# Rounding a gate input with a second activation, keeping gates as tanh, and a new order of all operations in a kernel of four blocks

## The reference

```python
# 1 state-space block (mamba), inner width 256, 16 states; it has its own layernorm and residual
h = layernorm(x, gamma, beta); xi, z = split(h @ W_in, 2)
u = silu(causal_conv4(xi) + b_conv)
dt_r, B, C = split(u @ W_x);  dt = softplus(dt_r @ W_dt + b_dt)
s[t] = exp(dt * A) * s[t-1] + dt * u * B[t]        # per channel, for each of 16 states
y = sum_over_states(s * C) + u * Dskip
block = x + (y * silu(z)) @ W_out
# 2 and 4: ffn with ternary weights, inner width 512
block = rmsnorm(gelu(rmsnorm(x) @ w_up_t)) @ w_down_t
# 3 minGRU, inner width 512, between the two ffns
x_in = silu(x @ W1 + b1); x_skip = silu(x @ W2 + b2)
z = sigmoid(x_in @ Wz + bz); ht = x_in @ Wh + bh
h[t] = (1 - z[t]) * h[t-1] + z[t] * ht[t]
block = (x_skip + h) @ Wo + bo
```

## Time and profile before

| | |
|---|---|
| median of 3 runs | 886.41 us (883.97 to 886.82) |
| profiled execution, its own time | 885.23 us |
| its span on the core | 883.4 us |
| PE, busy share of the span | 81% (719.2 us) |
| DVE | 80% (708.4 us) |
| ACT | 71% (629.6 us) |
| POOL | 67% (593.3 us) |
| mean granted TensorE clock | 0.895 |

### The profile page before, as it was taken

The page is one execution under the profiler, slowest core; times in us unless marked ns, Lnnn a source line. Parts: engine busy times, 40 slices in busy tenths (PEclk is TensorE's granted clock), DMA queues, the critical chain, the costliest instruction groups (busy, mean ns, idle before and its releaser), DMA issues. The chain is left out here.

```text
span 883.4 us, 12572 instructions
## 1 busy us (share of the span) xinstructions
PE 719.2 (81%) x4116; PEld 602.6 (68%) x4116; DVE 708.4 (80%) x1092; ACT 629.6 (71%) x942; POOL 593.3 (67%) x374
## 2 busy tenths in 40 slices
PE   5464675679979996999789987999699968997976
PEld 5343463568857785778777876788577857786765
DVE  3579887899979999799989997999799997844231
ACT  4654756678788968897798779887888477526322
POOL 3378847876787869776978787877868567515412
PEclk9755856889979999899989998999899988999995
DMA  2441221111211111121111111121112111000000
GB/s 46 123 168 45 65 60 48 56 42 50 60 47 39 60 45 52 40 71 48 49 50 56 52 55 41 50 61 48 45 42 60 49 36 36 13 1 1 12 1 13
DMA packets 35186, 42.80 MB, mean 48 GB/s; under 512 B 7457, under 2 KB 17074, under 8 KB 35122
## 3 DMA queue, kind: packets, MB, share of 16 engines
q1 hardware_dynamic: 35122, 42.00, 15.9%
HBM read 39.63 MB, written 2.36 MB: 48 GB/s over the span
## 5 line engine op out<-in xcount | busy, mean ns | idle before, releaser
L382 POOL TENSOR_TENSOR inflow<-dtu,b_all 128x1024 f32<-128x1024 f32 x127 | 311.8, 2457 | 121.7 <-DVE state L926 96.2
L1219 PE MATMUL y_ps<-ident,state 128*128 128x128 f32 x1024 | 154.4, 301 | 30.1 <-DVE state L934 30.1
L934 DVE TENSOR_TENSOR state<-state,c_ps 128x1024 f32<-128x1024 f32 x128 | 155.6, 1216 | 25.4 <-PE c_ps L1210 22.2
L1219 PEld LDWEIGHTS y_ps<-ident,state 128*128 128x128 f32 x1024 | 136.1, 157 | 47.4 <-DVE state L934 36.3
L923 DVE TENSOR_TENSOR_SCAN state<-dA,inflow 128x512 f32<-128x512 f32 x128 | 155.7, 1216 | 9.6 <-ACT dA L701 7.9
L926 DVE TENSOR_TENSOR_SCAN state<-dA,inflow 128x512 f32<-128x512 f32 x128 | 153.2, 1197 | 0.0
L701 ACT ACTIVATE dA<-dt,decay_c 128x512 f32<-128x512 f32 x128 | 88.0, 687 | 58.5 <-DVE state L923 50.9
L1114 PE MATMUL work<-in_hi,wzh_hi 128*128 128x512 f32 x256 | 105.9, 414 | 5.6 <-POOL in_lo L537 5.4
L1116 PE MATMUL work<-in_lo,wzh_hi 128*128 128x512 f32 x256 | 101.1, 395 | 0.0
L1115 PE MATMUL work<-in_hi,wzh_lo 128*128 128x512 f32 x256 | 100.8, 394 | 0.0
L703 ACT ACTIVATE dA<-dt,decay_c 128x512 f32<-128x512 f32 x128 | 87.3, 682 | 17.0 <-DVE state L926 16.6
(11 more groups left out here) (163 smaller groups left out, 1582.7 us busy)
## 6 DMA issues: line engine op xcount, KB each, us to landing
b_all<-b_scratch SPq DMA_DIRECT2D x128, 256.0 KB, 3.1
x_tok<-in_x SPq DMA_DIRECT2D x8, 256.0 KB, 3.8
out_x<-x_tok SPq DMA_DIRECT2D x8, 256.0 KB, 3.7
wide<-in_Wz SPq DMA_DIRECT2D x1, 1024.0 KB, 8.0
wide<-in_Wh SPq DMA_DIRECT2D x1, 1024.0 KB, 10.2
skip_f<-in_W SPq DMA_DIRECT2D x2, 256.0 KB, 5.1
dtu<-in_W_in SPq DMA_DIRECT2D x1, 256.0 KB
b_scratch<-gated SPq DMA_DIRECT2D x8, 32.0 KB, 1.6
```

The costliest lines, as they stand in the source:

```text
L382: eng.tensor_tensor(inflow[:, n % 2, :, :], dtu[:, :, :], b_all[:, n % RING, :].unsqueeze(1).broadcast_to([P, HALVES, SEQ]), ALU.mult).the ...
L934: dve.tensor_tensor(state[:, g % 3, :, :], state[:, g % 3, :, :], c_ps[:, :].unsqueeze(1).broadcast_to([P, HALVES, SEQ]), ALU.mult).then_i ...
L1219: last = pe.matmul(y_region(j, h), state[:, g % 3, h, cols(j)], ident[:, :], is_transpose=True, start=False, stop=(n == STATE - 1), skip_g ...
```

## The change

1. **Gate input.** The DVE copy into `in_hi` (32 of them) is gone. ACT runs the silu of `in0` to `in3` a second time, from the same PSUM bank, with the rounded tile as output. The bank is given free after the second. The semaphore `s_inhi` is gone: POOL's `in_lo` waits for the bank's release.
2. **Gates.** The second pass over the gate (32 on ACT) is gone; `gate` holds tanh t. Wh is halved once at the start (4 more ACT passes of 128x512), so that (t+1)*bank is z*(x_in@Wh). `keep` is -0.5t+0.5. The bias bh is taken out of the gated term: the scan starts at -bh instead of 0, and bh@Wo is added once to `bo_tok` (4 small matmuls and one DVE add at the start).
3. **Skip term.** The diagonal matrix (2 DVE instructions) is gone. ACT scales u by Dskip in place (`mix_ud`, 2 passes of 128x512 per unit, after `dtu` and x_dbl have read u), and PE adds it by eight transposes instead of eight matmuls.
4. **Order.** Every table of slots, the table of banks and `MOVED` are new. Unit 1 has exceptions of its own too. The load of x for unit b+2 stands 4 loads of B earlier in SP's queue.
5. Units are now described by (row, from, to, start) so that a unit could be part of a row. All eight are whole rows, so that the slices and the carry that go with it change nothing and no carry is issued.

The core of the diff:

```diff
+UNITS = (
+    (0, 0, 512, 0), (1, 0, 512, 16), (2, 0, 512, 32), (3, 0, 512, 48), (4, 0, 512, 64), (5, 0, 512, 80), (6, 0, 512, 96), (7, 0, 512, 112),
+)
...
             def round_wzh(k):
+                act.activation(wzh_f[:, k, FF:2 * FF], wzh_f[:, k, FF:2 * FF], ACT.Copy, scale=0.5).then_inc(s_halved, 1)
+                act.wait_ge(s_halved, k + 1)
                 act.activation(wzh_hi[:, k, :], wzh_f[:, k, :], ACT.Copy).then_inc(s_hizh, 1)
...
+            def mix_ud(b):
+
+                act.wait_ge(s_dtu, b + 1)
+                full(act, b, "xdbl")
+                for h in range(HALVES):
+                    last = act.activation(u[:, h, tok(b)], u[:, h, tok(b)], ACT.Identity, scale=skip_c[:, h:h + 1])
+                last.then_inc(s_ud, 1)
...
             def gru_in(t, j, r, s):
...
-                    act.activation(in_f[:, j, :], bank(p)[:, :], ACT.Silu, bias=b1_c[:, j:j + 1]
+                    read_by(act, r, s, "h3")
+                    act.activation(in_f[:, j, tok(t)], bank(p)[:, tok(t)], ACT.Silu, bias=b1_c[:, j:j + 1])
+                    act.activation(in_hi[:, j, tok(t)], bank(p)[:, tok(t)], ACT.Silu, bias=b1_c[:, j:j + 1]
                                    ).then_inc(*emptied(p))
...
-                evacuated(act, t, p)
-                act.activation(gate[:, j % 2, :], gate[:, j % 2, :], ACT.Copy, scale=0.5, bias=0.5).then_inc(s_gate1, 1)
...
-            def gru_in_hi(t, j, r, s):
-                evacuated(dve, t, "in%d" % j)
-                read_by(dve, r, s, "h3")
-                dve.tensor_copy(in_hi[:, j, :], in_f[:, j, :]).then_inc(s_inhi, 1)
...
-                dve.scalar_tensor_tensor(mixed[:, j, :], bank(p)[:, :], bh_c[:, j:j + 1], gate[:, j % 2, :],
+                dve.scalar_tensor_tensor(mixed[:, j, tok(t)], gate[:, j % 2, tok(t)], 1.0, bank(p)[:, tok(t)],
                                          ALU.add, ALU.mult).then_inc(*emptied(p))
...
+                first = nbh_c[:, j:j + 1] if FROM[t] == 0 else mixed[:, j, FROM[t] - 1:FROM[t]]
+                dve.tensor_tensor_scan(mixed[:, j, tok(t)], keep[:, j % 2, tok(t)], mixed[:, j, tok(t)], first,
                                        ALU.mult, ALU.add).then_inc(s_hid, 1)
...
-                        last = pe.matmul(y_region(j, h), u[:, h, cols(j)], diag[:, h, :],
+                        last = pe.matmul(y_region(j, h), u[:, h, cols(j)], ident[:, :], is_transpose=True,
                                          start=(j % 2 == 0 and h == 0), stop=False, skip_group_check=True)
```

428 lines of the change are left out of this document (239 added, 189 removed), and 120 rows, old and new, of tables (ACT_AT, BANK, DVE_AT, MOVED).

## The result

The changed kernel takes **870.4 us** (median of 4 runs, 870.2 to 874.7), the kernel before 885.2 in its 4: a ratio of 0.983, with a 95% interval of 0.980 to 0.986. The forecast was 879 and faster. The direction was right and the time lies in the range, but the gain, 14.8 us, is more than twice the 6.2 that were forecast. The profiled execution took 870.4 us, its span 868.6.

The account below looks back on a forecast made before the run. No engine alone was taken as the bound: DVE nearest, 8.9 us to spare per unit, PE and ACT close behind. Sum: 885.2 + 4.9 (silu block) - 11.0 (gate stretch) + 2.0 (start) - 2.1 (end) = 879 us; range 858 to 895.

Parts of the forecast that it names:

- the start: Before the third unit: first scan 4.7 us late at 41.4, partly swallowed by ACT's wait for GRU weights; +2.0 us.
- fourth rival: TensorE's clock falls around the skip term as transposes replace matmuls; 898 by itself, 892 with the other terms; chance 0.03.
- Silu block: ACT's silus between table loads, steps 12 to 13: twelve instead of eight, +0.7 us in each of seven units, +4.9 us.
- Gate stretch: PE's eight banks of gate matmuls behind the silus: DVE's three waits, 1.83 us, go in six units; -11.0 us.
- PE's lead: In the gate stretch: earlier in_lo lets PE start z1 near 385.9 instead of 389.23, about 3 us ahead.
- Skip term: PE's adding of u times Dskip: the same 16 records per unit, 1.95 us, so nothing.
- Gate copies: ACT's second pass over the gate: loses 20.2 us of ACT work, costed at nothing outside the silu block.
- End: Behind the last scan: gate matmuls now ahead of both last states, DVE's 2.07 us wait goes; -2.1 us.
- Casts: DVE's 32 casts, 3.7 us per unit inside the silu block, where ACT is as late: nothing by themselves.
- the first: Rival: DVE decides everywhere, seven units give back 3.7 us each; 859 us, chance 0.18.
- The third: Rival: silu block slower, step 13's scan 1.7 us late in seven units, +11.9, no waits removed; 899 us, chance 0.22.

Follow-up runs that it names:

- new_none: The changed kernel's order with the three edits undone (casts, gate copies and diagonal matrix back): 899.9 us, ratio 1.016 to the kernel before.
- old_start: The three edits in the old order, but state-space operations of units 0 and 1 in the changed kernel's slots: 900.7 us, ratio 1.015.
- old_all: The changed kernel's three edits with every table (slots, banks, load of x) of the kernel before: 892.4 us, ratio 1.008.
- The fillers: Matmuls of zeros added where PE waits in units 0 to 5: kernel before 873.2 us (885.2 without), changed kernel 867.0 (870.4 without).
- old_skip: The kernel before with one edit, u scaled by Dskip on ACT and added by transposes: 886.7 us, ratio 0.999.
- new_diag: The changed kernel with only the skip term undone (diagonal matrix and matmuls again): 876.0 us, ratio 0.988 to the kernel before.
- old_silu: The kernel before with one edit, the second silu in place of the casts, all slots as they were: 894.0 us, ratio 1.007.
- new_gates: The changed kernel with only the gates undone (copy pass, Wh not halved, bh inside the gated term): 874.6 us, ratio 0.987.
- new_cast2: The changed kernel with all four casts on DVE again and POOL's in_lo in its old slots: 895.9 us, ratio 1.011.
- mix_fill: The changed kernel with inputs 2 and 3 cast by DVE, in_lo2 moved later, and six matmuls of zeros per unit 0 to 5: 867.9 us, ratio 0.977.
- fill6: The changed kernel with six matmuls of zeros behind d.up1 of units 0 to 5, where PE waits: 867.0 us, ratio 0.976.

## Why the prediction came out as it did

**The step that failed is the start.** I had: first scan at 41.4, then "+2.0 us" once the wait for the GRU's weights has swallowed a part, and nothing more until the middle. The stretch up to the third unit moved by -6.7 us instead. The first half held: the first scan came at 40.7, the weights' wait of 5.68 us is gone, and at step 3 the kernel is 2.8 us behind (57.7 against 55.0). Then it gained 9.4 us up to the third unit, where I had booked +0.7 for one silu block.

In unit 0 (82.1 to 75.4 us) DVE is idle for 4.8 us less and busy for 2.0 less (its two `m_vv` operations took 3.9 us and take 0.4, its two `keep` operations 1.6 more). From step 3 on, it waits 3.9 us before, 3.2 of them for C rows; after, not at all. new_none shows that this is the order's work, without any edit, and old_start that the order of the state-space operations is enough. In unit 1 (89.8 to 85.9) DVE is busy for 6.2 us less, of which 4.9 are unit 0's casts, and idle for 2.2 more. The order alone gives 0.5 us there (new_none, 89.3) and the edits in the old order 0.8 (old_all, 89.0); together they give 4.0, and why was not followed further. I had read the order of units 0 and 1 only up to step 3, though the change gave both exceptions of their own.

**There was no term for the clock.** The fillers put it at 8.6 us for units 2 to 6 of the kernel before (471.2 to 462.6) and 3.8 for the changed one (467.6 to 463.8). The difference, 4.8 us, is more than these units gained (3.6); with fillers in both, the changed kernel is 1.2 us *slower* in them. These are single profiled runs; by the medians of the whole, with twelve fillers per unit in one kernel and six in the other, the clock's share in the gain is 14.8 less 6.2, 8.6 us. That 6.2 is also what I had forecast is chance: the start still gives its part, and I had it as a loss.

My fourth rival had the clock the wrong way round: it looked at the skip term itself, and the falls come some 45 us later (541.6 in unit 5 of the kernel before), behind waits of PE. Why the skip edit made that fall longer in the old order is open; in old_skip it begins near 537 us, behind a wait of 2.27 us for `n_tok`. The Trainium skill, "TensorE: Matmul & The Clock Gate", section "Part 4: PE-mode transpose", has transposes not count as busy, and the direction fits (0.78 for 0.85); but the place is another, and new_diag at the same mean clock, 0.904, speaks against it.

**The middle, by steps.** Units 2 to 6 together, from the scans of both kernels:

| steps | what is due there | moved, us | with fillers in both | my terms |
|---|---|---|---|---|
| 0 to 5 | gate stretch, skip term | -6.1 | -5.9 | -9.2 |
| 5 to 8 | | +1.0 | +1.4 | |
| 8 to 11 | most of the clock's falls | -9.0 | -4.3 | |
| 11 to 13 | silu block | +9.1 | +8.7 | +3.5 |
| 13 to 16 | | +1.4 | +1.4 | |
| all | | -3.6 | +1.2 | -5.7 |

**Silu block, +4.9.** Right mechanism, half the size. It measured 1.5 us per unit in old_silu and 1.4 to 2.0 in units 2 to 6 of the changed kernel (12.1 to 12.7 against 10.6 us), about +11 for seven units. The silus run at 0.59, and at 0.70 for the last four; my 0.56 came from two silus alone. The estimate of 0.61 us that the prediction took from the Trainium skill, "ScalarE: Activation LUTs", section "What ACT_TABLE_LOAD costs", was nearer for the first eight. For the banks that are held longer I had added 0.4 us; PE's two waits for them measure 1.21 and 0.74.

**Gate stretch, -11.0.** The waits went in part, and for another reason than mine in their largest part: of the 6.1 us, five times 0.9 = 4.5 are the skip term, as new_diag shows. What is left for PE's lead is some 0.3 us per unit, where I had 1.83. The two `mixed` scans are still stretched, 4.50 us for the pair at 321.10.

**Skip term, nothing.** Wrong, -0.9 us per unit. I wrote that "the same 16 records per unit" would stay. The trace of the kernel before had the answer, eight transposes and eight matmuls 4 us apart:

```profile
308.40 1.03 PE L1228 MATMUL work<-ident,z_tok 128*128 128x128 f32 x8
...
312.00 1.95 PE L1237 MATMUL work<-wout_sb,gated 128*128 128x128 f32 x16
```

**Gate copies, nothing.** Nothing shows a gain against the kernel before, where 14 to 15 takes 4.7 us with the copies. In the new order they would cost 0.6 us per unit (new_gates), so the new order needs the edit.

**End, -2.1.** The size came, 2.07 us at the output gate of 2.8 in all, but not by my mechanism: the wait for `y_ps` is still 2.22 us, and other work went from in front of it. That the two have the same size is luck.

**Casts, nothing by themselves.** Right in the old order (a wait of 3.97 us took their place). In the new one all four could not be put back for less than 20 us, in new_cast2 13 of them by POOL's slots; two of the four could (mix_fill and fill6 are 0.9 us apart).

Of the rivals, the first (DVE everywhere, a unit under 91.5 us) fell: units 3, 5 and 6 take 92.0 to 92.7, units 2 and 4 more. The third was right about the place, its mark and nearly the price (11.9), and wrong that nothing would pay for it. That the sum for units 2 to 7 came close, -6.8 against -5.4, is luck: the silu block cost 6 us more and the gate stretch gave 3 less than I had, while 9 us that I had no term for came in steps 8 to 11 (units 2 to 6). About half of these are the clock; what the rest is was not followed.
